# Four partial sums of a job: three merges, or one strided reduce of a PSUM bank

## The chip, the cores and the metric

The kernel runs on one core of a Trainium2 chip (trn2). The metric is the time of one launch on the device in microseconds. It was measured in three runs.

## The reference

A recommendation model. For each of 512 samples, 39 embeddings of 16 numbers are gathered from 39 tables. They go through three layers of a compressed interaction network, then through three dense layers. Cut to what matters here, with m = 39 fields, h = the previous layer's units (39, then 128) and 128 units out:

```python
prev = x                                   # [b, 39, 16]
for k in range(3):
    z = jnp.einsum('bmd,bhd->bdmh', x, prev).reshape(b, D, m * h)
    t = jnp.einsum('bdc,co->bdo', z, ws[k]) + bs[k]
    t = jnp.transpose(t, (0, 2, 1))
    norm = jnp.sqrt(jnp.sum(t * t, axis=(-2, -1), keepdims=True))
    t = t / norm
    logit.append(t)
    prev = t
```

For layers 1 and 2 this is, for each sample and embedding column, the sum over 39 fields m of x[m] times (prev row times the weight matrix of field m).

## The kernel before

The 512 samples are 16 chunks of 32; a chunk has 32 x 16 = 512 rows, four tiles of 128. A **job** is one tile of one chunk in layer 1 or 2; there are 128 jobs (`NJ`), interleaved: in iteration `it`, four jobs of layer 1 for chunk `it`, then four of layer 2 for chunk `it - 1`. So the loop repeats every 8 jobs.

In a job, TensorE multiplies the tile of prev with the weights of four fields at a time into one PSUM bank of 512 columns (four fields of 128 units), each bank with three matmuls (low by high, high by low and high by high halves, lines 554 to 556). Ten banks make the 39 fields. Five banks (19 fields) are the A half: ScalarE scales each field's 128 columns by that field's x column (`scale_bank`, line 441), into `sums` for the first bank and into `scaled` for the rest, and GpSimd adds them to `sums` (`add_bank`, line 333). The A banks have a ring of two PSUM banks, and TensorE is `LEAD` = 7 banks ahead with them.

The other five banks are the D half: 20 fields (`D_FIELDS`), numbered u = 0 to 19 here, field u in bank u // 4 at columns 128 x (u % 4), over a ring of three PSUM banks (`bank_d`). VectorE takes each field with one scalar_tensor_tensor (`add_field`, line 756): bank columns times the x column plus `sums[u % 4]`. It can begin field 0 only when GpSimd's four adds of the same job are done (`a_added`, line 749), since both use the four partial sums in `sums`. Field u of 4 and over waits for field u - 4.

At the end of a job four partial sums are left and have to become one. Fields 17 and 18 (`LEFT`) write their results back to their own columns of the bank. Field 19 adds to partial sum 0, which already has field 17's result. The **three merges** (`merge`, line 775) are: step 0, partial sum 0 = partial sum 0 + field 17's columns; step 1, field 18's columns = these + partial sum 3; step 2, partial sum 0 = partial sum 0 + field 18's columns. VectorE's program order is, by hand: field 18, steps 0 and 1, field 19, field 0 of the next job, step 2, field 1, and so on. TensorE waits for the semaphore `merged` in two places: before it writes the bank three D banks later (line 582), and before it transposes the total (`turn_sums`, line 591) into `turned`.

After a chunk's four tiles ScalarE adds the bias (`finish`), VectorE sums values and squares (`sum_values`, `sum_squares`, lines 779 and 783, tensor_reduce of 512 columns to 32), TensorE sums squares over partitions, ScalarE takes the root, and VectorE makes the reciprocal in four short steps (lines 793 to 804), placed between fields 1 to 4 of a later job. `make_prev` (line 821) then writes the next layer's prev, ScalarE copies its high half (`high`, line 481), and GpSimd makes the low half (`low`, line 338). ScalarE's program order has `high` between two scale_bank calls. Layer 0 goes by products of pairs of fields: VectorE multiplies them (`make_pairs`, line 734), and TensorE sums them with 14 matmuls a chunk (line 619). Every queue's order is written out by hand.

Of the kernel before, what the change touches and what calls it, by code (L numbers as in the profile page):

```python
# [8 lines left out]
UNITS = 128  # L9
# [27 lines left out]
PER_BANK = 4  # L37
A_BANKS = 5
BANKS = -(-FIELDS // PER_BANK)
D_BANKS = BANKS - A_BANKS  # L40
A_FIELDS = A_BANKS * PER_BANK - 1
D_FIELDS = FIELDS - A_FIELDS
ADDS = A_BANKS - 1


LEFT = (D_FIELDS - 3, D_FIELDS - 2)
TOTAL = (D_FIELDS - 4) % PER_BANK
MERGES = 3
A_RING, D_RING = 2, 3
SUMS = 5  # L50

# [8 lines left out]
NJ = len(JOBS)  # L60
# [76 lines left out]
def cin_kernel(nc, idx_in, base_in, table, ctx_t, w0a, w0b, w1, w2, b0, b1, b2,  # L137
               w_top1, b_top1, w_top2, b_top2, w_top3, out):
    f32, f32r, i32 = mybir.dt.float32, mybir.dt.float32r, mybir.dt.int32
    ALU, ACT, AX = mybir.AluOpType, mybir.ActivationFunctionType, mybir.AxisListType  # L140
# [4 lines left out]
    with ExitStack() as ctx:  # L145
        def sb(name, shape, dt=f32):
            return ctx.enter_context(nc.sbuf_tensor(name, shape, dt))

        def pb(name):
            return ctx.enter_context(nc.psum_tensor(name, [128, 512], f32))  # L150

        def sem(name):
            return ctx.enter_context(nc.semaphore(name))
# [29 lines left out]
        sums = sb("sums", [128, SUMS, PER_BANK, UNITS])  # L183
# [17 lines left out]
        bank_d = [pb(f"bank_d{n}") for n in range(D_RING)]  # L201
# [30 lines left out]
        d_added = sem("d_added")  # L232
        merged = sem("merged")
# [29 lines left out]
        def d_fields_of(d):  # L263
            return min(PER_BANK, D_FIELDS - d * PER_BANK)

        def d_count(n, d):

            return n * D_FIELDS + min(PER_BANK * (d + 1), D_FIELDS)

        def x_of(c, q, m):  # L270
            return x_col[:, c % 3, q, m:m + 1]
# [274 lines left out]
        def _(pe):  # L546
            def three_terms(bank, k, c, q, m, count):

                at = slice(q * COLS, (q + 1) * COLS)
                lo, hi = prev_lo[k][:, c % 2, at], prev_hi[k][:, c % 2, at]  # L550
                to = bank[:, 0:count * UNITS]
                w_h = w_hi[k][:, m:m + count, :].rearrange("p m u -> p (m u)")
                w_l = w_lo[k][:, m:m + count, :].rearrange("p m u -> p (m u)")
                nc.tensor.matmul(to, lo, w_h, start=True, stop=False)  # L554
                nc.tensor.matmul(to, hi, w_l, start=False, stop=False)  # L555
                return nc.tensor.matmul(to, hi, w_h, start=False, stop=True)  # L556
# [17 lines left out]
            def bank_for_dve(n, d):  # L574
                k, c, q = JOBS[n]
                at = D_BANKS * n + d
                if n == 0:
                    pe.wait_ge(w_lo_made[1], len(W_PIECES[1]))
                if at >= D_RING:
                    was, bank = divmod(at - D_RING, D_BANKS)  # L580
                    if bank == D_BANKS - 1:
                        pe.wait_ge(merged, MERGES * (was + 1))
                    else:
                        pe.wait_ge(d_added, d_count(was, bank))
                three_terms(bank_d[at % D_RING], k, c, q, A_FIELDS + d * PER_BANK,
                            d_fields_of(d)).then_inc(d_ready, 1)

            def turn_sums(n):

                k, c, q = JOBS[n]  # L590
                pe.wait_ge(merged, MERGES * (n + 1))
                if q == 0 and n >= TILES:
                    k, c, _ = JOBS[n - 1]
                    pe.wait_ge(squared, FINISH_NO[k, c] + 1)
                nc.tensor.transpose(turned[:, q * COLS:(q + 1) * COLS], sums[:, n % SUMS, TOTAL, :],  # L595
                                    identity[:, :]).then_inc(turn_done, 1)
# [59 lines left out]
            for n in range(NJ):  # L656
                d = a = 0
                for place, whose in enumerate(PATTERN):
# [10 lines left out]
                    if (n, place) in PAIR_MATMULS_AT:  # L669
                        c, tiles = PAIR_MATMULS_AT[n, place]  # L670
# [20 lines left out]
            for n in range(2):  # L691
                for k in range(3):
                    top1(n, k)
            turn_sums(NJ - 1)
            for k in range(3):
                top1(2, k)
# [22 lines left out]
        def _(dve):  # L719
# [19 lines left out]
            def taken(n, u):  # L739
                d, i = divmod(u, PER_BANK)  # L740
                return bank_d[(D_BANKS * n + d) % D_RING][:, i * UNITS:(i + 1) * UNITS]

            def add_field(n, u):
                k, c, q = JOBS[n]
                d, i = divmod(u, PER_BANK)
                if i == 0:
                    dve.wait_ge(d_ready, D_BANKS * n + d + 1)
                if u < PER_BANK:
                    dve.wait_ge(a_added, ADDS * (n + 1))
                elif u < D_FIELDS - 1:  # L750
                    dve.wait_ge(d_added, n * D_FIELDS + u + 1 - PER_BANK)
                else:
                    dve.wait_ge(merged, MERGES * n + 1)
                total = sums[:, n % SUMS, TOTAL if u == D_FIELDS - 1 else u % PER_BANK, :]

                nc.vector.scalar_tensor_tensor(  # L756
                    out=taken(n, u) if u in LEFT else total, in0=taken(n, u), scalar=x_of(c, q, A_FIELDS + u),
                    in1=total, op0=ALU.mult, op1=ALU.add).then_inc(d_added, 1)

            def merge(n, step):  # L760

                first, second = LEFT
                total = sums[:, n % SUMS, TOTAL, :]
                other = sums[:, n % SUMS, (D_FIELDS - 1) % PER_BANK, :]
                if step == 0:
                    dve.wait_ge(d_added, n * D_FIELDS + first + 1)
                    out, in0, in1 = total, taken(n, first), total
                elif step == 1:
                    dve.wait_ge(d_added, n * D_FIELDS + second + 1)
                    out, in0, in1 = taken(n, second), taken(n, second), other  # L770
                else:
                    dve.wait_ge(d_added, (n + 1) * D_FIELDS)
                    dve.wait_ge(merged, MERGES * n + 2)
                    out, in0, in1 = total, taken(n, second), total
                nc.vector.tensor_tensor(out=out, in0=in0, in1=in1, op=ALU.add).then_inc(merged, 1)  # L775

            def sum_values(k, c):
                dve.wait_ge(biased, FINISH_NO[k, c] + 1)
                nc.vector.tensor_reduce(dsum[:, k, :], bdim(t[:, k, :]), AX.X, ALU.add).then_inc(values_summed, 1)
# [34 lines left out]
            def make_prev(b, k, c):  # L814
                dve.wait_ge(r_step, (b + 1) * R_STEPS)
                if c:
                    dve.wait_ge(prev_lo_made[k], c)
                if c >= 2:

                    dve.wait_ge(d_ready, D_BANKS * (JOB_AT[k, c - 2, TILES - 1] + 1))  # L820
                nc.vector.tensor_tensor(out=bdim(prev[:, k - 1, :]), in0=bdim(t[:, k - 1, :]),
                                        in1=r[:, k - 1, :].unsqueeze(2).to_broadcast([128, CB, EMB]),
                                        op=ALU.mult).then_inc(prev_made[k], 1)
# [4 lines left out]
                                    in1=w0b_sb[0:PAIR_ROWS, full, :], op=ALU.add).then_inc(w0_folded, 1)  # L828
            last = PAIR_TILES - 1
            nc.vector.tensor_tensor(out=w0_sb[0:FIELDS, last, :], in0=w0_sb[0:FIELDS, last, :],  # L830
                                    in1=w0b_sb[0:FIELDS, last, :], op=ALU.add).then_inc(w0_folded, 1)
# [19 lines left out]
            for n in range(NJ):  # L851
                for u in range(D_FIELDS):
                    add_field(n, u)
                    if u == LEFT[1]:
                        merge(n, 0)
                        merge(n, 1)
                    if u == 0 and n:
                        merge(n - 1, 2)
                    for b, (items, _, _, at) in enumerate(NORMS):
                        if at and at[0] == n:  # L860
                            since = u - at[1]
                            if since in (0, 1, 2, 3):
                                reciprocal_step(b, since)
                            prevs = [(k + 1, c) for k, c in items if k < 2]
                            if since in (4, 5) and since - 4 < len(prevs):
                                make_prev(b, *prevs[since - 4])
                            if since == 6:
                                features(b)
                    for k, c, _, at in FINISHES:
                        if at == (n, u):  # L870
                            sum_values(k, c)
                        if at and at == (n, u - 3):
                            sum_squares(k, c)
                    if (n, u) in PAIRS_AT:
                        make_pairs(*PAIRS_AT[n, u])
            merge(NJ - 1, 2)
            sum_values(2, CHUNKS - 1)
            sum_squares(2, CHUNKS - 1)
            for step in range(R_STEPS):
# [61 lines left out]
```

## Time and profile before

| | us |
|---|---|
| median of 3 runs | 1101.58 |
| lowest, highest | 1101.01, 1102.05 |
| profiled execution | 1101.28 |
| its span, first to last instruction | 1099.6 |

Mean granted TensorE clock of the span: 0.992. Line numbers in a profile are those of the kernel. A row of a timeline gives start and duration in us; where several alike follow each other they are merged as "x4". Instructions of one engine overlap, so the distance from one start to the next is often shorter than a duration. In square brackets stands how long the engine was idle before and whom it waited for.

### The profile page before, as it was taken

What the parts mean: (1) busy time and instruction counts of PE and PEld (TensorE: products, weight loads), DVE (VectorE), ACT (ScalarE), POOL (GpSimd) and SP (SyncE); (2) the same over time, 40 slices, a digit from 0 to 9 for tenths busy, and PEclk for the clock granted to TensorE, in tenths of its full rate; (3) what the DMA queues carried; (4) which work ended last, traced back from release to release, by engine and by line L of the source; (5) the groups of instructions that cost most, each with busy time, mean ns of one, the idle gap of its engine ahead of it and who ended that gap; (6) DMA issues with size and microseconds to landing.
All of it is one profiled execution on the core that took longest, in us unless ns stands there. A gap on an engine that the chain in (4) does not pass through costs nothing.

```text
span 1099.6 us, 17904 instructions
## 1 busy us (share of the span) xinstructions
PE 1052.5 (96%) x4394; PEld 794.1 (72%) x4394; DVE 969.0 (88%) x3317; ACT 780.5 (71%) x2628; POOL 866.9 (79%) x726
## 2 busy tenths in 40 slices
PE   0798999999999999999999999999999999999999
PEld 0366687777778787777778777777777777788773
DVE  2467799998999999999999999999999999899892
ACT  3266586877768687776868777786868777688762
POOL 5587798888889888888888888888888888577660
PEclk9899999999999999999999999999999999999999
DMA  6503040110303011030303002030301203000000
GB/s 228 131 13 73 2 118 7 35 41 3 73 3 73 2 35 42 5 71 3 73 2 71 5 11 66 3 73 2 74 2 20 56 3 73 0 2 1 1 1 1
DMA packets 56735, 41.20 MB, mean 37 GB/s; under 512 B 37915, under 2 KB 40859, under 8 KB 56502
## 3 DMA queue, kind: packets, MB, share of 16 engines
q1 hardware_dynamic: 49145, 32.17, 12.5%
q10 hardware_dynamic: 2365, 6.60, 1.7%
q0 software_dynamic: 5120, 1.29, 1.3%
q8 instruction: 35, 0.57, 0.2%
q14 instruction: 70, 0.57, 0.2%
HBM read 38.09 MB, written 1.94 MB: 36 GB/s over the span
## 4 chain that ended last, share of the span: by engine, by line
PE 67%; POOL 21%; issue 6%; ACT 4%; DMA 1%; DVE 0%; SPq 0%; POOLq 0%; ACTq 0%
POOL sums L333 17%; PE bank_a L554 10%; PE bank_d L554 9%; PE acc L619 9%; PE bank_d L555 9%; PE bank_d L556 9%; PE bank_a L556 9%; PE bank_a L555 9%; POOL gathered L320 4%; ACT scaled L441 2%; PE turned L595 1%; ACT sums L441 1%; PE bank_a L684 1%; DMA x_pairs<-x_scratch 1%; PE bank_d L708 1%
## 5 line engine op out<-in xcount | busy, mean ns | idle before, releaser
L333 POOL TENSOR_TENSOR sums<-sums,scaled 128x512 f32<-128x512 f32 (+1 forms) x512 | 642.8, 1256 | 154.0 <-ACT scaled L441 119.3
L756 DVE SCALAR_TENSOR_TENSOR sums<-bank_d,x_col,sums 128x128 f32<-128x128 f32 x2304 | 654.8, 339 | 74.4 <-PE bank_d L556 58.8
L441 ACT ACTIVATE scaled<-bank_a,x_col 128x128 f32<-128x128 f32 x1920 | 550.6, 382 | 152.9 <-PE bank_a L556 144.4
L554 PE MATMUL bank_d<-w_hi,prev_lo 128*128 128x512 f32 x640 | 286.1, 447 | 1.2 <-DVE sums L775 0.9
L554 PE MATMUL bank_a<-w_hi,prev_lo 128*128 128x512 f32 (+1 forms) x640 | 274.5, 429 | 12.0 <-POOL prev_lo L338 6.3
L556 PE MATMUL bank_d<-w_hi,prev_hi 128*128 128x512 f32 x640 | 253.3, 396 | 0.0
L555 PE MATMUL bank_d<-w_lo,prev_hi 128*128 128x512 f32 x640 | 253.0, 395 | 0.0
L556 PE MATMUL bank_a<-w_hi,prev_hi 128*128 128x512 f32 (+1 forms) x640 | 246.2, 385 | 0.0
L555 PE MATMUL bank_a<-w_lo,prev_hi 128*128 128x512 f32 (+1 forms) x640 | 245.9, 384 | 0.0
L441 ACT ACTIVATE sums<-bank_a,x_col 128x128 f32<-128x128 f32 x512 | 146.1, 370 | 88.3 <-PE bank_a L556 88.3
L320 POOL DMA_INDIRECT gathered<-in_table,idx x160 | 177.2, 1107 | 31.9 <-issue 21.7
L554 PEld LDWEIGHTS bank_a<-w_hi,prev_lo 128*128 128x128 f32 x640 | 120.6, 188 | 66.0 <-issue 20.9
L554 PEld LDWEIGHTS bank_d<-w_hi,prev_lo 128*128 128x128 f32 x640 | 121.0, 189 | 42.0 <-DVE sums L756 8.7
L555 PEld LDWEIGHTS bank_a<-w_lo,prev_hi 128*128 128x128 f32 x640 | 121.1, 189 | 37.2 <-issue 13.7
L555 PEld LDWEIGHTS bank_d<-w_lo,prev_hi 128*128 128x128 f32 x640 | 121.7, 190 | 29.7 <-issue 10.8
L556 PEld LDWEIGHTS bank_d<-w_hi,prev_hi 128*128 128x128 f32 x640 | 121.0, 189 | 28.9
L556 PEld LDWEIGHTS bank_a<-w_hi,prev_hi 128*128 128x128 f32 x640 | 120.8, 189 | 22.7
L619 PE MATMUL acc<-z,w_sb 117*128 117x512 f32 (+1 forms) x224 | 115.9, 605 | 0.7 <-issue 0.7
L734 DVE TENSOR_TENSOR z<-x_pairs 117x1024 f32<-117x1024 f32 x64 | 106.8, 1672 | 5.1 <-DMA x_pairs<-x_scratch 4.9
L756 DVE SCALAR_TENSOR_TENSOR bank_d<-bank_d,x_col,sums 128x128 f32<-128x128 f32 x256 | 78.8, 348 | 0.0
L775 DVE TENSOR_TENSOR sums<-bank_d,sums 128x128 f32<-128x128 f32 x256 | 71.3, 279 | 0.4 <-DVE sums L756 0.4
L619 PEld LDWEIGHTS acc<-z,w_sb 117*128 117x128 f32 (+1 forms) x224 | 42.4, 195 | 15.0 <-issue 6.0
(59 smaller groups left out, 484.7 us busy)
## 6 DMA issues: line engine op xcount, KB each, us to landing
x_pairs<-x_scratch SPq DMA_DIRECT2D x141, 156.0 KB
x_pairs<-x_scratch SPq DMA_DIRECT2D x78, 78.0 KB
gathered<-in_table,idx POOLq DMA_INDIRECT x160
w_raw<-in_w ACTq DMA_DIRECT2D x2, 768.0 KB, 7.2
x_scratch<-gathered SPq DMA_DIRECT2D x16, 72.0 KB
w_raw<-in_w ACTq DMA_DIRECT2D x1, 1024.0 KB, 5.7
w_raw<-in_w ACTq DMA_DIRECT2D x1, 896.0 KB
w_raw<-in_w ACTq DMA_DIRECT2D x1, 832.0 KB
```

The source lines that it names most:

```text
L320: nc.gpsimd.indirect_dma_start(out=gathered[0:n, c % 2, j, :], out_offset=None, in_=table[:, :], in_offset=bass.IndirectOffsetOnAxis(ap=id ...
L333: nc.gpsimd.tensor_tensor(out=sums[:, n % SUMS, 0:w, :], in0=sums[:, n % SUMS, 0:w, :], in1=scaled[:, a - 1, 0:w, :], op=ALU.add).then_inc ...
L441: op = nc.scalar.activation(to[:, i, :], bank_a[at % A_RING][:, i * UNITS:(i + 1) * UNITS], ACT.Copy, scale=x_of(c, q, a * PER_BANK + i))
L554: nc.tensor.matmul(to, lo, w_h, start=True, stop=False)
L555: nc.tensor.matmul(to, hi, w_l, start=False, stop=False)
L556: return nc.tensor.matmul(to, hi, w_h, start=False, stop=True)
L595: nc.tensor.transpose(turned[:, q * COLS:(q + 1) * COLS], sums[:, n % SUMS, TOTAL, :], identity[:, :]).then_inc(turn_done, 1)
L619: mm = nc.tensor.matmul(acc0[:, :], w0_sb[0:rows, tile, :], z0[0:rows, tile, :], start=(tile == 0), stop=(tile == PAIR_TILES - 1))
L684: return nc.tensor.matmul(tops[n][:, :], w[:, n * 128:(n + 1) * 128], x, start=(k == 0), stop=(k == 3))
L734: nc.vector.tensor_tensor(out=z0[0:rows, tiles[0]:tiles[0] + count, :], in0=x_rep[0:rows, :].unsqueeze(1).to_broadcast([rows, count, ROWS] ...
L756: nc.vector.scalar_tensor_tensor(out=taken(n, u) if u in LEFT else total, in0=taken(n, u), scalar=x_of(c, q, A_FIELDS + u), in1=total, op0 ...
L775: nc.vector.tensor_tensor(out=out, in0=in0, in1=in1, op=ALU.add).then_inc(merged, 1)
```

## The change

The last four fields of a job, 16 to 19, all write their results into their own columns of the job's last bank. Each still adds its partial sum. The three merges are gone. In their place a single tensor_reduce reads the bank with the order of dimensions turned, so that the four columns of a unit, 128 columns apart, are added, and writes the 128 totals to partial sum 0. It stands where the third merge stood, behind field 0 of the next job. Field 19 now adds partial sum 3 and waits for field 15 as others wait for theirs. `merged` counts one for a job.

```diff
-LEFT = (D_FIELDS - 3, D_FIELDS - 2)
-TOTAL = (D_FIELDS - 4) % PER_BANK
-MERGES = 3
+assert D_FIELDS % PER_BANK == 0
+TOTAL = 0
...
                     if bank == D_BANKS - 1:
-                        pe.wait_ge(merged, MERGES * (was + 1))
+                        pe.wait_ge(merged, was + 1)
...
-                pe.wait_ge(merged, MERGES * (n + 1))
+                pe.wait_ge(merged, n + 1)
...
-                elif u < D_FIELDS - 1:
+                else:
                     dve.wait_ge(d_added, n * D_FIELDS + u + 1 - PER_BANK)
-                else:
-                    dve.wait_ge(merged, MERGES * n + 1)
-                total = sums[:, n % SUMS, TOTAL if u == D_FIELDS - 1 else u % PER_BANK, :]
+                total = sums[:, n % SUMS, u % PER_BANK, :]
 
                 nc.vector.scalar_tensor_tensor(
-                    out=taken(n, u) if u in LEFT else total, in0=taken(n, u), scalar=x_of(c, q, A_FIELDS + u),
+                    out=taken(n, u) if u >= D_FIELDS - PER_BANK else total, in0=taken(n, u), scalar=x_of(c, q, A_FIELDS + u),
                     in1=total, op0=ALU.mult, op1=ALU.add).then_inc(d_added, 1)
 
-            def merge(n, step):
...
-                nc.vector.tensor_tensor(out=out, in0=in0, in1=in1, op=ALU.add).then_inc(merged, 1)
+            def merge(n):
+
+                dve.wait_ge(d_added, (n + 1) * D_FIELDS)
+                bank = bank_d[(D_BANKS * n + D_BANKS - 1) % D_RING]
+                nc.vector.tensor_reduce(sums[:, n % SUMS, TOTAL, :], bank.rearrange("p (i u) -> p u i", u=UNITS),
+                                        AX.X, ALU.add).then_inc(merged, 1)
...
                     add_field(n, u)
-                    if u == LEFT[1]:
-                        merge(n, 0)
-                        merge(n, 1)
                     if u == 0 and n:
-                        merge(n - 1, 2)
+                        merge(n - 1)
...
-            merge(NJ - 1, 2)
+            merge(NJ - 1)
```

## Rows read from the trace of the kernel before

**Rows 1.** The page, part 1: busy time and instructions of each engine.

```profile
PE 1052.5 (96%) x4394; PEld 794.1 (72%) x4394; DVE 969.0 (88%) x3317; ACT 780.5 (71%) x2628; POOL 866.9 (79%) x726
```

**Rows 2.** Busy us by stretches of one period: stretch, length, engines, clock, DMA.

```profile
454.90:486.50 31.60, 31.48 (x142) 25.32 (x141) 31.23 (x118) 25.92 (x90) 28.13 (x24) 1.00 0.29 64
486.50:494.40 7.90, 7.90 (x33) 5.65 (x31) 7.27 (x21) 5.93 (x19) 7.03 (x7) 1.00 0.04 5
494.40:510.20 15.80, 15.80 (x64) 11.40 (x63) 15.63 (x51) 9.25 (x33) 13.37 (x12) 1.00 0.02 2
510.20:518.00 7.80, 7.80 (x38) 6.21 (x37) 5.96 (x22) 6.58 (x22) 5.50 (x6) 1.00 0.01 1
sum 63.10, PE 62.98 PEld 48.58 DVE 60.09 ACT 47.68 POOL 54.03; mean PE 15.74 PEld 12.15 DVE 15.02 ACT 11.92 POOL 13.51
```

**Rows 3.** Waits from 195 to 985 us: total us, times, longest.

```profile
ACT prev_hi L481 <- DVE prev L821: 13.0, 13, 1.8
...
PEld bank_a L554 <- ACT scaled L441: 12.1, 26, 0.6
...
DVE sums L756 <- POOL sums L333: 4.8, 12, 0.7
```

**Rows 4.** Timeline of VectorE, 533 to 538 us: start, duration, instruction.

```profile
533.02 0.28 DVE L775 TENSOR_TENSOR sums<-bank_d,sums 128x128 f32<-128x128 f32 x1
...
533.42 0.34 DVE L756 SCALAR_TENSOR_TENSOR sums<-bank_d,x_col,sums 128x128 f32<-128x128 f32 x1
534.09 0.35 DVE L756 SCALAR_TENSOR_TENSOR sums<-bank_d,x_col,sums 128x128 f32<-128x128 f32 x1 [0.33 <-POOL sums L333]
534.36 0.28 DVE L775 TENSOR_TENSOR sums<-bank_d,sums 128x128 f32<-128x128 f32 x1
534.56 0.60 DVE L756 SCALAR_TENSOR_TENSOR sums<-bank_d,x_col,sums 128x128 f32<-128x128 f32 x2
...
536.87 0.68 DVE L821 TENSOR_TENSOR prev<-t,small 128x512 f32<-128x512 f32 x1
```

**Rows 5.** Timeline of ScalarE in two periods, around the copy of prev.

```profile
474.48 0.63 ACT L481 ACTIVATE prev_hi<-prev 128x512 fp32r<-128x512 f32 x1 [0.92 <-DVE prev L821]
...
537.58 0.63 ACT L481 ACTIVATE prev_hi<-prev 128x512 fp32r<-128x512 f32 x1 [0.92 <-DVE prev L821]
538.12 0.86 ACT L441 ACTIVATE scaled<-bank_a,x_col 128x128 f32<-128x128 f32 x3
```

**Rows 6.** Timeline of TensorE, 538 to 539.6 us.

```profile
538.28 0.39 PE L555 MATMUL bank_d<-w_lo,prev_hi 128*128 128x512 f32 x1
538.51 0.40 PE L556 MATMUL bank_d<-w_hi,prev_hi 128*128 128x512 f32 x1
539.03 0.50 PE L554 MATMUL bank_a<-w_hi,prev_lo 128*128 128x512 f32 x1
```

**Rows 7.** Groups by line and shape, whole span: busy us, mean ns, idle before.

```profile
L775 DVE TENSOR_TENSOR sums<-bank_d,sums 128x128 f32<-128x128 f32 x256 | 71.3, 279 | 0.4 <-DVE sums L756 0.4
...
L779 DVE TENSOR_REDUCE dsum<-t 128x32 f32<-128x512 f32 x48 | 32.4, 674 | 9.7 <-ACT t L465 9.7
...
L821 DVE TENSOR_TENSOR prev<-t,small 128x512 f32<-128x512 f32 x32 | 21.7, 678 | 0.0
```

**Rows 8.** Timeline of VectorE at a reduce, 518 to 519.4 us.

```profile
518.30 0.67 DVE L783 TENSOR_REDUCE ssq<-squares 128x32 f32<-128x512 f32 x1
518.90 0.35 DVE L756 SCALAR_TENSOR_TENSOR bank_d<-bank_d,x_col,sums 128x128 f32<-128x128 f32 x1
519.16 0.28 DVE L775 TENSOR_TENSOR sums<-bank_d,sums 128x128 f32<-128x128 f32 x1
```

**Rows 9.** The pair products: ns min/median/max, first and last start, shapes.

```profile
L734 DVE TENSOR_TENSOR z<-x_pairs x64: 671/1386/2690, 35.4 to 947.2; 117x1024 f32<-117x1024 f32 x48, 78x512 f32<-78x512 f32 x16
```

**Rows 10.** Timeline of VectorE and TensorE behind the last job.

```profile
1075.86 0.29 DVE L775 TENSOR_TENSOR sums<-bank_d,sums 128x128 f32<-128x128 f32 x1 [0.22 <-DVE sums L756]
...
1078.94 0.27 PE L595 MATMUL turned<-identity,sums 128*128 128x128 f32 x1
```

More of the change, by code:

```diff
@@ L749, in add_field @@
                     dve.wait_ge(a_added, ADDS * (n + 1))
-                elif u < D_FIELDS - 1:
+                else:
                     dve.wait_ge(d_added, n * D_FIELDS + u + 1 - PER_BANK)
-                else:
-                    dve.wait_ge(merged, MERGES * n + 1)
-                total = sums[:, n % SUMS, TOTAL if u == D_FIELDS - 1 else u % PER_BANK, :]
+                total = sums[:, n % SUMS, u % PER_BANK, :]
                 nc.vector.scalar_tensor_tensor(
-                    out=taken(n, u) if u in LEFT else total, in0=taken(n, u), scalar=x_of(c, q, A_FIELDS + u),
+                    out=taken(n, u) if u >= D_FIELDS - PER_BANK else total, in0=taken(n, u), scalar=x_of(c, q, A_FIELDS + u),
                     in1=total, op0=ALU.mult, op1=ALU.add).then_inc(d_added, 1)
-            def merge(n, step):
[L762 to L774, printed above, removed]
-                nc.vector.tensor_tensor(out=out, in0=in0, in1=in1, op=ALU.add).then_inc(merged, 1)
+            def merge(n):
[3 more added lines that the diff above has]
+                                        AX.X, ALU.add).then_inc(merged, 1)
             def sum_values(k, c):
```

## The prediction

> **What bounds the kernel now.** I read the busy times of the engines first, then the same by stretches of one period of the loop, then the waits of the long middle, then the order of instructions in the place where these waits meet. TensorE is busy 96% of the span and VectorE 88% [rows 1]. The loop repeats every 8 jobs: the copy that makes the high half of prev starts at 474.48 and again at 537.58, 63.10 us later [rows 5]. In such a period TensorE is busy 62.98 of 63.10 us and VectorE 60.09 [rows 2]. So TensorE leaves nothing to win in the middle: 0.12 us a period by that row, some 2 us in all. Another engine matters only where TensorE waits for it.
>
> The stretches [rows 2] show where that is. In the first 31.6 us (four jobs) VectorE is busy 31.23 us, and TensorE loses its 0.12 us there. The waits name the place: ScalarE waits about 1 us for prev once in a period (13.0 us, 13 times), VectorE 0.4 us for GpSimd's sums (4.8 us, 12 times), and TensorE's weight loads for bank_a wait for ScalarE's scaling [rows 3].
>
> Put in order, this is one chain. GpSimd's last add of a job lets VectorE begin field 0 of that job, at 534.09 after 0.33 us of waiting. Behind field 0 stand, in program order, the third merge of the job before (534.36), field 1 (534.56), more fields with the reciprocal steps between them, and make_prev at 536.87 [rows 4]. ScalarE sits idle 0.92 us until prev is there, copies it at 537.58, and only then, at 538.12, scales the bank that TensorE wants back [rows 5]. TensorE's next matmul into bank_a starts at 539.03, 0.52 us behind the one before it, where the steady distance is 0.23 [rows 6]. So 0.29 us of TensorE is lost there now, and whatever delays VectorE between 534.36 and 536.87 should add to it one for one. In this place VectorE is on the path, although TensorE is the bound elsewhere.
>
> **The change, part by part.** Instructions of VectorE overlap, so I count from start to start. The first two merges of a job take 533.02 to 533.42, the third 534.36 to 534.56: 0.20 us each, 0.60 us a job [rows 4], for 128 jobs (384 merges, of which the 256 that write sums have one row [rows 7]). Removed: 0.60 us a job.
>
> Added: one tensor_reduce a job that reads 512 columns and writes 128. The nearest rows are this kernel's own reduces of 512 columns to 32, 674 ns each [rows 7]; one starts at 518.30 and its successor at 518.90, 0.60 us [rows 8]. So 0.60 out and 0.60 in: VectorE's busy time gains nothing.
>
> Those reduces read SBUF side by side; the new one reads PSUM, with the four terms of each sum 128 columns apart. From below: a 128-column add is 279 ns and a 512-column multiply 678 [rows 7], so 384 more columns cost 399 ns, 1.04 ns a column, and 512 columns 0.53 us. From above: the pair products are the only VectorE work here whose rate changes; their median is 1386 ns and the slowest of the same shape takes 2690 [rows 9], about a factor of two. At twice the time per column the reduce would take 0.53 + 0.60 = 1.13 us. I take 0.60, from the row that is the same operation with the same count read: the multiply of 512 columns, which has PSUM among its inputs (r, each value read 16 times), is 678 ns against the reduce's 674 out of SBUF alone [rows 7], so neither PSUM nor a pattern other than side by side has a price in these rows.
>
> The Trainium skill, in "Advanced Engine Details and Errata", section PSUM Cachelines, says that PSUM's lines are 8 bytes and that a pattern that isn't contiguous slows matmuls significantly; of VectorE it says nothing there. The Trainium skill's "VectorE: DVE Perf Modes", section "Mode 1× (REGULAR) — the baseline", has it the other way: this mode assumes nothing and takes strange strides and PSUM operands. No row of before shows a strided read of PSUM.
>
> Fields 16 and 19 now write their bank in place of sums. A field that writes sums takes 534.09 to 534.36 [rows 4], one that writes the bank 518.90 to 519.16 [rows 8]: no cost. TensorE's waits on merged count to 1 in place of 3 and are met by the same event, the last step of the job. That event stays at its distance from field 18: before, field 18, two merges, field 19, field 0 and a merge are 0.26 + 0.20 + 0.20 + 0.26 + 0.26 + 0.20 = 1.38 us; after, 3 x 0.26 + 0.60 = 1.38. DMA queues, ScalarE and GpSimd issue what they issued.
>
> What moves is work past field 0. Before, two merges stood ahead of field 0 of the next job and one behind it; after, none ahead and 0.60 us behind. Where field 0 waits for nothing, it starts 0.40 us earlier and field 1 when it did. Where field 0 waits for GpSimd, it can't start earlier; the two merges used to be done before the wait was over, and now 0.40 us more stands behind it. In the stretch of rows 4: field 19 would start at 533.02, field 0 still at 534.09, the reduce at 534.36, field 1 at 534.96 and not 534.56, make_prev at 537.27, the high half at 537.98, the matmul at 539.43. Queued behind the reduce on VectorE are field 1, the reciprocal steps and make_prev; ScalarE waits for make_prev, TensorE for ScalarE. None of them has slack, so TensorE loses 0.40 us more there, has no idle time later in the period to make it up [rows 2], and the period becomes 63.5 us.
>
> How often: field 0's wait is there 12 times and ScalarE's 13 times [rows 3]. I take 13: 13 x 0.40 = 5.2 us.
>
> The ends: in the last job the last merge starts at 1075.86 and takes 0.29 us, and the transpose that reads it starts at 1078.94 [rows 10], behind matmuls that don't need it, so over 2 us of cover remain there, and in that job the order gives 1.29 us from field 18 before (0.26 + 0.40 + 0.34 + 0.29) and 1.27 after (0.26 + 0.34 + 0.67). At the start I count nothing. Sum: 1101.28 us of the profiled execution (span 1099.6) + 5.2 = 1106.5; the median of the runs, 1101.58, is 0.3 above it, so 1106.8.
>
> **The rivals.** *Covered after all.* The reduce goes at the rate of the rows and the shift is taken up, for instance because GpSimd, with fewer writes to SBUF beside it, reaches its last add sooner. For it: 0.60 against 0.60. Against: ScalarE's wait and TensorE's late start stand in the rows. It gives 1101.6, within a microsecond.
>
> *The strided read is slow.* At 1.13 us a reduce, VectorE has 8 x 0.53 = 4.2 us a period more and 3.0 free (63.10 - 60.09), so the period grows by at least 1.2. By stretches [rows 2], as three banks carry little work from one to the next, the excess over the time there is: 31.23 + 4 x 0.53 - 31.60 = 1.75; 7.27 + 0.53 - 7.90, none; 15.63 + 2 x 0.53 - 15.80 = 0.89; none in the last: 2.6 us. Over 15 periods this is 18 to 40 us, 1120 to 1141. From 0.98 us a reduce on (0.60 + 3.0 / 8) VectorE is the bound of the whole period; in the first four jobs, where it has 0.37 us free, a tenth more a reduce is enough. I set it at 1134; a rate between, 0.8 us, adds at rows 4's place 0.60 and in the full stretches 0.4, some 8 to 15 us. If the Trainium skill's rule on PSUM lines held for VectorE, it would be this case.
>
> *Faster.* If the reduce came in at 0.53 us, and TensorE won back its 0.12 us and part of its 0.29 us in each period because no shift came, it gives 1098. Against it: only two instructions a job fewer, and their time is replaced.
>
> *It doesn't do what it says*: 384 merges become 128 reduces by the code; this is not open.
>
> **How the numbers follow.** Forecast 1106.8 (0.5% slower), chance 0.45, its own range 1104 to 1110; covered 0.20; slow read 0.30, from 1110 to 1143; faster 0.05. The low end, 1100.5, takes in the covered case, the high end, 1141, most of the slow read. A measurement of this kernel can tell about 0.2%, 2.2 us, from no change. Slower by more than that: 0.45 and 0.30, less a little, 0.73. Within it 0.22. Faster 0.05.
>
> **What would show it.** A mean of the reduce near 0.67 us and its successor 0.60 us behind its start confirm the price; 1.2 us is the slow read. In the place of rows 4, field 1 starting 0.87 us behind field 0 and not 0.47, ScalarE waiting 1.3 us for prev and not 0.92, TensorE's gap before bank_a 0.9 us and not 0.52 confirm the shift, and a period of 63.5 us the sum; VectorE's busy time in a period should stay near 60. If the reduce costs 0.60 us and the period stays at 63.1, the step on the shift is wrong. If TensorE waits for bank_d all over the first four jobs, the slow read decides.

## The result and the profile after

The changed kernel takes 1106.48 us (median of 6 runs, 1104.44 to 1106.99), the kernel before beside it 1101.39 us. The ratio is 1.0042, 95% interval 1.0029 to 1.0055: slower by 0.4%. The forecast was 1106.8. The profiled execution has a span of 1104.5 us, 4.9 more than before.

First the page: busy time and instructions of each engine, then the groups of the reduce and of the fields that now write their bank (busy us, mean ns of one, idle before).

```profile
PE 1055.1 (96%) x4394; PEld 792.2 (72%) x4394; DVE 969.0 (88%) x3061; ACT 780.6 (71%) x2628; POOL 867.1 (79%) x726
...
L753 DVE SCALAR_TENSOR_TENSOR bank_d<-bank_d,x_col,sums 128x128 f32<-128x128 f32 x512 | 145.3, 347 | 14.5 <-PE bank_d L555 14.5
...
L761 DVE TENSOR_REDUCE sums<-bank_d 128x128 f32<-128x512 f32 x128 | 86.7, 677 | 0.0
```

256 instructions fewer on VectorE, and its busy time is 969.0 us to the digit, as in [rows 1]. The strided reduce out of PSUM takes 677 ns, the one out of SBUF 674 [rows 7].

One period after, from busy time by stretches (length; busy us of PE, PEld, DVE, ACT, POOL), against the sum in [rows 2]:

```profile
458.05:521.55 63.50, 63.23 (x272) 48.53 (x271) 60.03 (x191) 47.68 (x164) 53.96 (x46) 1.00 0.15 33
```

VectorE's 60.03 us are the 60.09 of before, and the period is 0.40 us longer. The waits of the middle, as [rows 3]:

```profile
PEld bank_a L553 <- ACT scaled L440: 12.4, 25, 0.6
PEld bank_d L553 <- DVE sums L753: 11.8, 35, 0.6
DVE sums L753 <- POOL sums L332: 9.0, 24, 1.2
...
ACT prev_hi L480 <- DVE prev L808: 16.7, 12, 1.8
```

ScalarE waits 1.4 us a time for prev and not 1.0. VectorE's field 0 waits for GpSimd twice in a period now, 24 times and not 12. The place itself, on VectorE's timeline, as [rows 4]:

```profile
535.65 1.12 DVE L753 SCALAR_TENSOR_TENSOR bank_d<-bank_d,x_col,sums 128x128 f32<-128x128 f32 x4
537.22 0.35 DVE L753 SCALAR_TENSOR_TENSOR sums<-bank_d,x_col,sums 128x128 f32<-128x128 f32 x1 [0.45 <-POOL sums L332]
537.49 0.68 DVE L761 TENSOR_REDUCE sums<-bank_d 128x128 f32<-128x512 f32 x1
538.08 0.60 DVE L753 SCALAR_TENSOR_TENSOR sums<-bank_d,x_col,sums 128x128 f32<-128x128 f32 x2
...
540.39 0.68 DVE L808 TENSOR_TENSOR prev<-t,small 128x512 f32<-128x512 f32 x1
```

The four fields run through, field 0 waits, and between it and field 1 there are now 0.86 us (537.22 to 538.08) where there were 0.47. make_prev starts 3.17 us behind field 0 and not 2.78. ScalarE and TensorE behind it, as [rows 5, 6]:

```profile
477.62 0.63 ACT L480 ACTIVATE prev_hi<-prev 128x512 fp32r<-128x512 f32 x1 [1.32 <-DVE prev L808]
...
541.11 0.63 ACT L480 ACTIVATE prev_hi<-prev 128x512 fp32r<-128x512 f32 x1 [1.33 <-DVE prev L808]
...
540.92 0.40 PE L555 MATMUL bank_a<-w_hi,prev_hi 128*128 128x512 f32 x1
541.39 0.50 PE L553 MATMUL bank_d<-w_hi,prev_lo 128*128 128x512 f32 x1
541.73 0.39 PE L554 MATMUL bank_d<-w_lo,prev_hi 128*128 128x512 f32 x1
541.96 0.40 PE L555 MATMUL bank_d<-w_hi,prev_hi 128*128 128x512 f32 x1
542.56 0.50 PE L553 MATMUL bank_a<-w_hi,prev_lo 128*128 128x512 f32 x1 [0.21 <-ACT scaled L440]
542.90 0.39 PE L554 MATMUL bank_a<-w_lo,prev_hi 128*128 128x512 f32 x1
...
541.39 0.19 PEld L553 LDWEIGHTS bank_d<-w_hi,prev_lo 128*128 128x128 f32 x1 [0.51 <-DVE sums L753]
```

ScalarE waits 1.33 us and not 0.92, the copies are 63.49 us apart and not 63.10. TensorE, at 0.23 us a matmul elsewhere, has 0.47, 0.34, 0.60 and again 0.34 us here between starts. The last row is the weight load of the matmul at 541.39: it waited for VectorE to give back its bank.

### The profile page after: what moved, and what is told of

It reads as the page before. It is cut to its first block, busy times and chain, and to the rows that moved or that the text cites. A ratio compares the mean times of both kernels' runs of the same rounds, so it can differ in the third digit from the quotient of the medians.

```text
span 1104.5 us, 17520 instructions
## 1 busy us (share of the span) xinstructions
PE 1055.1 (96%) x4394; PEld 792.2 (72%) x4394; DVE 969.0 (88%) x3061; ACT 780.6 (71%) x2628; POOL 867.1 (79%) x726
## 4 chain that ended last, share of the span: by engine, by line
PE 60%; POOL 21%; issue 5%; DVE 5%; ACT 5%; DMA 2%; SPq 0%; POOLq 0%; ACTq 0%; DVEq 0%
POOL sums L332 16%; PE acc L618 9%; PE bank_a L553 8%; PE bank_d L553 8%; PE bank_a L555 8%; PE bank_a L554 8%; PE bank_d L555 8%; PE bank_d L554 8%; POOL gathered L319 5%; ACT scaled L440 4%; DVE sums L753 2%; DVE prev L808 1%; DVE sums L761 1%; PE turned L594 1%; PE bank_a L683 1%
## 5 line engine op out<-in xcount | busy, mean ns | idle before, releaser
L753 DVE SCALAR_TENSOR_TENSOR sums<-bank_d,x_col,sums 128x128 f32<-128x128 f32 x2048 | 580.1, 337 | 64.8 <-PE bank_d L555 46.1
L753 DVE SCALAR_TENSOR_TENSOR bank_d<-bank_d,x_col,sums 128x128 f32<-128x128 f32 x512 | 145.3, 347 | 14.5 <-PE bank_d L555 14.5
L761 DVE TENSOR_REDUCE sums<-bank_d 128x128 f32<-128x512 f32 x128 | 86.7, 677 | 0.0
```

The costliest lines, as they stand in the source:

```text
L753: nc.vector.scalar_tensor_tensor(out=taken(n, u) if u >= D_FIELDS - PER_BANK else total, in0=taken(n, u), scalar=x_of(c, q, A_FIELDS + u), ...
L761: nc.vector.tensor_reduce(sums[:, n % SUMS, TOTAL, :], bank.rearrange("p (i u) -> p u i", u=UNITS), AX.X, ALU.add).then_inc(merged, 1)
```

## The experiments

The theory of the place says: the reduce costs as much as the merges, and the loss is that 0.40 us more of it stand behind a field 0 that waits. Its rival says that the reduce costs by itself, by its length, its reads or its hold on the bank. The periods below are the distance of ScalarE's copies of prev's high half in jobs 8k+2, as in [rows 5]. They are read from one period of each trace; a table behind the last experiment has thirteen periods of every kernel. The kernel before was measured beside each set of runs; its median was 1102.49 us beside the first four experiments, 1102.10 beside the next four and 1101.28 beside the last.

**The reduce ahead of field 0, in one job of a period.**

```diff
+AHEAD = range(10, 128, 8)
...
                 for u in range(D_FIELDS):
+                    if u == 0 and n in AHEAD:
+                        merge(n - 1)
                     add_field(n, u)
-                    if u == 0 and n:
+                    if u == 0 and n and n not in AHEAD:
                         merge(n - 1)
```

> The changed kernel with the reduce moved ahead of field 0 in one job of each period (jobs 10, 18, ... 122, the ones whose field 0 waits for GpSimd before make_prev); everywhere else it stays behind field 0. Theory of the place (what stands behind that field 0 is on the path): 0.60 us less behind field 0 than in the changed kernel, of which 0.40 is the loss of the change and 0.20 comes off the 0.29 us that TensorE lost in the kernel before; period 63.5 to 62.9 us, 13 x 0.60 = 7.8 us off 1106.5, so 1098 to 1100; ScalarE's wait for prev 0.7 us. Rival (the reduce itself costs, by its length, by how long it holds the bank or by its reads): 128 reduces are still there, 1105 to 1107.

Measured: 1102.01 us, ratio to before 0.9998 (0.9989 to 1.0007), so not the 1098 to 1100 expected. The loss of the change is gone with 15 of 128 reduces moved, which the rival can't explain. The further gain didn't come. VectorE's timeline of this kernel says why:

```profile
534.05 1.12 DVE L754 SCALAR_TENSOR_TENSOR bank_d<-bank_d,x_col,sums 128x128 f32<-128x128 f32 x4
535.21 0.69 DVE L762 TENSOR_REDUCE sums<-bank_d 128x128 f32<-128x512 f32 x1
535.81 0.86 DVE L754 SCALAR_TENSOR_TENSOR sums<-bank_d,x_col,sums 128x128 f32<-128x128 f32 x3
...
538.38 0.68 DVE L809 TENSOR_TENSOR prev<-t,small 128x512 f32<-128x512 f32 x1
```

Four fields start 1.03 us apart in all (4 x 0.26), so the reduce could start at 535.08 and starts at 535.21: it waits for field 19 right ahead of it. And field 0 carries no mark of a wait here: VectorE, not GpSimd, is last to come. It left job 8k+1 late, since field 0 waits there too, which is the second wait a period in the list above.

**The same with merges.** The diff is the one above in the kernel before, with `merge(n - 1, 2)`.

> The kernel before with the third merge moved ahead of field 0 in the same jobs (10, 18, ... 122). Theory of the place: 0.20 us less behind field 0, all of it inside the 0.29 us that TensorE loses there; period 63.1 to 62.9 us, 13 x 0.20 = 2.6 us off 1101.4, so 1098 to 1099.5. Rival (TensorE is the bound of the kernel before and VectorE's order is covered): 1101 to 1102.

Measured: 1099.08 us, ratio 0.9974 (0.9964 to 0.9983), the copies 62.88 us apart:

```profile
474.32 0.63 ACT L482 ACTIVATE prev_hi<-prev 128x512 fp32r<-128x512 f32 x1 [0.91 <-DVE prev L822]
...
537.20 0.64 ACT L482 ACTIVATE prev_hi<-prev 128x512 fp32r<-128x512 f32 x1 [0.70 <-DVE prev L822]
```

A kernel whose TensorE is busy 96% gets 0.26% faster by moving one 0.20 us instruction of VectorE past another, once in eight jobs. That is the mechanism with the sign turned.

**The same amount behind field 0, without a reduce.**

```diff
+            def extra(n):
+                dve.wait_ge(merged, MERGES * n + 2)
...
+                for half in range(2):
+                    nc.vector.tensor_tensor(out=spare[:, half, :], in0=taken(n, LEFT[1]),
+                                            in1=sums[:, n % SUMS, (D_FIELDS - 1) % PER_BANK, :],
+                                            op=ALU.add).then_inc(spare_made, 1)
...
+                    if u == 0 and n in MORE:
+                        extra(n - 1)
                     if u == 0 and n:
                         merge(n - 1, 2)
```

> The kernel before with two more 128-column adds, results unused, between field 0 and the third merge in the same jobs (10, 18, ... 122); no reduce of a bank. They put 0.60 us behind field 0 as the change does, with merges. Theory of the place: as the changed kernel, period 63.5 us, 13 x 0.40 = 5.2 us more, 1106 to 1107.5. Rival (the reduce itself costs): VectorE has 3 us free in a period, 0.40 more in one job is covered, 1101 to 1102.

Measured: 1107.48 us, ratio 1.0053 (1.0041 to 1.0065). The copies are 63.47 us apart, ScalarE waits 1.31 to 1.37 us:

```profile
476.69 0.63 ACT L484 ACTIVATE prev_hi<-prev 128x512 fp32r<-128x512 f32 x1 [1.37 <-DVE prev L836]
...
540.16 0.63 ACT L484 ACTIVATE prev_hi<-prev 128x512 fp32r<-128x512 f32 x1 [1.31 <-DVE prev L836]
```

The change's loss is copied with merges alone, over thirteen periods 5.38 us with them and 5.27 with the change.

**The same adds elsewhere in the period** (`MORE = range(15, 128, 8)`).

> The kernel before with the same two more adds at the same distance behind field 0, but in jobs 15, 23, ... 127, whose field 0 waits for TensorE's bank and behind which VectorE is idle. Theory of the place: TensorE's next need of these banks is 2 us off, nothing is lost, 1101 to 1102. Rival (any VectorE time added costs): 5 to 6 us as in the other kernel with more adds, 1106 to 1107.

Measured: 1103.12 us, ratio 1.0009 (1.0000 to 1.0019), the copies 63.12 us apart. The same work in a job where field 0 waits for TensorE costs 0.02 us in this period and not 0.37, and 0.7 us over thirteen periods and not 5.4. By the medians it is 0.6 us slower, at the edge of what can be told. The 1101 to 1102 expected was missed, mostly because the kernel before itself was at 1102.49 in this set.

```profile
475.77 0.63 ACT L484 ACTIVATE prev_hi<-prev 128x512 fp32r<-128x512 f32 x1 [0.97 <-DVE prev L836]
...
538.89 0.64 ACT L484 ACTIVATE prev_hi<-prev 128x512 fp32r<-128x512 f32 x1 [0.94 <-DVE prev L836]
```

**Field 0 without its wait, with merges and with the reduce.** The same edit in both kernels:

```diff
+SHORT = [n for n in range(9, 128) if n % 8 in (1, 2)]
...
-                w = a_fields_of(a)
+                w = a_fields_of(a) if a < A_BANKS - 1 or n not in SHORT else 1
```

> The kernel before with GpSimd's last add cut from 3 fields to 1 in two jobs of each period (9, 10, 17, 18, ...), so two fields' contributions of one bank are left out of those jobs' sums. It frees field 0 of these jobs about 0.6 us earlier, before VectorE gets to it. Theory of the place: field 0 waits no more, TensorE's 0.29 us goes, period 62.8 to 62.9 us, 1097 to 1099. Its main use is as the base for the next kernel.

> The changed kernel with the same cut of GpSimd's last add in the same jobs, the same contributions left out. Theory of the place: the 0.40 us was lost only because field 0 waited; without that wait field 0 starts 0.40 us earlier than with the merges and field 1 when it did, so this kernel is as fast as the kernel before with the same cut, within 1.5 us. Rival (the reduce costs by itself, or the distance behind field 0 costs with or without a wait): 5 us slower than it.

Measured: 1096.42 us with merges, ratio 0.9950 (0.9936 to 0.9963), and 1097.83 with the reduce, ratio 0.9957 (0.9943 to 0.9970). The difference of 5.1 us between the kernels has come down to 1.4, inside the 1.5 expected, though not to nothing. The first kernel gained a little more than expected; the part on TensorE's gap below has the reason. The copies of prev with merges, then with the reduce:

```profile
472.50 0.64 ACT L482 ACTIVATE prev_hi<-prev 128x512 fp32r<-128x512 f32 x1 [0.79 <-DVE prev L822]
...
535.23 0.63 ACT L482 ACTIVATE prev_hi<-prev 128x512 fp32r<-128x512 f32 x1 [0.49 <-DVE prev L822]
```

```profile
472.84 0.63 ACT L481 ACTIVATE prev_hi<-prev 128x512 fp32r<-128x512 f32 x1 [0.65 <-DVE prev L809]
...
535.65 0.63 ACT L481 ACTIVATE prev_hi<-prev 128x512 fp32r<-128x512 f32 x1 [0.65 <-DVE prev L809]
```

These are 62.73 and 62.81 us. With the reduce field 0 comes to its turn 0.40 us earlier, and a rest of the wait for GpSimd is left. In this trace the four fields start at 530.59, so field 0 could start 4 x 0.26 us later, at 531.63; it starts at 531.76:

```profile
530.59 1.13 DVE L754 SCALAR_TENSOR_TENSOR bank_d<-bank_d,x_col,sums 128x128 f32<-128x128 f32 x4
531.76 0.35 DVE L754 SCALAR_TENSOR_TENSOR sums<-bank_d,x_col,sums 128x128 f32<-128x128 f32 x1
```

13 times those 0.13 us are 1.7. In the two traces thirteen periods differ by 1.8 us (816.06 and 817.86), the medians by 1.4.

**The stride by itself.**

```diff
-bank.rearrange("p (i u) -> p u i", u=UNITS)
+bank.rearrange("p (u i) -> p u i", u=UNITS)
```

> The changed kernel with the reduce reading four columns side by side in place of four columns 128 apart, so it adds the wrong terms: the four partial sums of a unit are not what is added. All theories that have the strided read at full rate: the reduce takes 677 ns as before and the time is that of the changed kernel, 1105 to 1107.5. Rival (the stride has a price in it): the reduce gets shorter than 677 ns.

Measured: 1106.47 us, ratio 1.0038 (1.0026 to 1.0050), and the reduce is as long as before:

```profile
L761 DVE TENSOR_REDUCE sums<-bank_d 128x128 f32<-128x512 f32 x128 | 87.0, 679 | 0.0
```

A stride of 128 columns in PSUM had no price in this fp32 reduce of VectorE: 677 ns strided, 679 side by side, and the kernel isn't faster with the second.

**Both jobs with a wait mended.** `AHEAD = [n for n in range(9, 128) if n % 8 in (1, 2)]` in the first experiment's kernel.

> The changed kernel with the reduce ahead of field 0 in two jobs of each period, 8k+1 and 8k+2. With one job (8k+2) the period was 63.1 and not the 62.9 expected: the trace has VectorE come 0.2 us late out of job 8k+1, where field 0 waits for GpSimd too, and the reduce wait 0.1 us for field 19 right ahead of it. Theory: with the job before it mended as well, field 1 of job 8k+2 starts 0.2 us behind GpSimd's add less than before, period 62.9 to 63.0, 1099 to 1101. Rival (what is lost is the reduce's wait for field 19, twice now): 63.2 and over, 1103.

Measured: 1097.76 us beside 1102.10, ratio 0.9961 (0.9947 to 0.9974), faster than the 1099 to 1101 expected. The copies are 62.97 us apart, as expected, and ScalarE waits 0.79 us:

```profile
473.11 0.63 ACT L481 ACTIVATE prev_hi<-prev 128x512 fp32r<-128x512 f32 x1 [0.77 <-DVE prev L809]
...
536.08 0.63 ACT L481 ACTIVATE prev_hi<-prev 128x512 fp32r<-128x512 f32 x1 [0.79 <-DVE prev L809]
```

The idea of the change, placed right, beats both kernels, by less than the medians say. Of the 4.3 us between them thirteen periods explain 1.4. Another part is TensorE's clock and not the order of work: the mean granted clock was 0.994 in all five runs of this kernel, and 0.991 or 0.992 in all eleven of the kernel before beside it. In the kernel before that difference goes with 1.6 us (last section). The remaining 1.3 us stay open.

**Ahead of field 0 in every job.** `AHEAD = range(1, 128)`.

> The changed kernel with the reduce ahead of field 0 in every job from 1 on. In the two jobs of a period with a wait of field 0 this gained (period 62.97 against 63.50); in the other six the reduce now waits some 0.12 us for field 19 right ahead of it, and VectorE is nearly full there. Theory: that wait costs only where VectorE holds TensorE up, at most six times 0.12 in a period; VectorE's 0.6 us of idle time in the middle absorbs part: period 63.0 to 63.4, 1098 to 1103, no faster than with two jobs. Rival (the place behind field 0 costs in every job): faster than with two jobs, under 1097.

Measured: 1099.88 us, ratio 0.9984 (0.9975 to 0.9993), faster than before. By the ratios it gains less than with two jobs, but the periods don't show that: the copies are 63.00 us apart here and 62.97 there, and thirteen periods take 819.79 us here and 819.87 there. In the middle of the loop the two are the same, and the ratio of the other has its clock in it. So the reduce's place in the other six jobs costs nothing and gains nothing that these runs can tell. The reduce, whose group had no idle time before it in the changed kernel, now has 4.4 us of it:

```profile
L762 DVE TENSOR_REDUCE sums<-bank_d 128x128 f32<-128x512 f32 x128 | 88.5, 692 | 4.4
```

**Thirteen periods of every kernel.** One trace each, from a copy of prev's high half near 158 us to the one thirteen periods later. The rows are those of the kernel before, then of the changed kernel; the table has the same distance for all.

```profile
158.00 0.63 ACT L481 ACTIVATE prev_hi<-prev 128x512 fp32r<-128x512 f32 x1 [0.62 <-DVE prev L821]
...
979.28 0.63 ACT L481 ACTIVATE prev_hi<-prev 128x512 fp32r<-128x512 f32 x1 [0.73 <-DVE prev L821]
```

```profile
159.13 0.63 ACT L480 ACTIVATE prev_hi<-prev 128x512 fp32r<-128x512 f32 x1 [0.98 <-DVE prev L808]
...
985.68 0.63 ACT L480 ACTIVATE prev_hi<-prev 128x512 fp32r<-128x512 f32 x1 [1.13 <-DVE prev L808]
```

| kernel | from, to (us) | thirteen periods | against before |
|---|---|---|---|
| before | 158.00, 979.28 | 821.28 | |
| changed | 159.13, 985.68 | 826.55 | +5.27 |
| reduce ahead, one job | 159.63, 980.45 | 820.82 | -0.46 |
| third merge ahead, one job | 158.59, 977.70 | 819.11 | -2.17 |
| two more adds in the place | 158.21, 984.87 | 826.66 | +5.38 |
| two more adds elsewhere | 158.86, 980.87 | 822.01 | +0.73 |
| merges, without the wait | 158.05, 974.11 | 816.06 | -5.22 |
| reduce, without the wait | 157.93, 975.79 | 817.86 | -3.42 |
| reduce, side by side | 159.08, 986.19 | 827.11 | +5.83 |
| reduce ahead, two jobs | 157.26, 977.13 | 819.87 | -1.41 |
| reduce ahead, every job | 158.38, 978.17 | 819.79 | -1.49 |

## Why the prediction was right, and where it wasn't exact

*The price of the reduce.* Taken as 0.60 us from start to start, between bounds of 0.53 and 1.13. It is 0.59 (537.49 to 538.08), and VectorE's busy time didn't move. The choice by the row of the same operation held; the slow read, given 0.30, is refuted by the 677 ns and by the experiment on the stride. The Trainium skill's rule on PSUM's lines ("Advanced Engine Details and Errata", section PSUM Cachelines), which speaks of matmuls, doesn't carry over to VectorE here: 677 ns against 679. The section "Mode 1× (REGULAR) — the baseline" of "VectorE: DVE Perf Modes" in the Trainium skill, which takes strange strides and PSUM operands, agrees with these two numbers.

*The work that moves past field 0.* The step that made the forecast. Field 1 at 0.87 us behind field 0 was expected, it is 0.86; ScalarE's wait of 1.3 us is 1.33; the period of 63.5 us is 63.49. The kernel with extra adds in this place (1107.48) copies the loss without a reduce, the one with them elsewhere (1103.12) doesn't, and without field 0's wait 1.4 us are left of 5.1.

*TensorE's gap.* One gap of 0.92 us before bank_a was expected. There are two, 0.47 us before bank_d and 0.60 before bank_a. VectorE's delay hits TensorE first through the bank it has to give back, then through ScalarE. The path through bank_d was not in the prediction; the sum is the same, since both carry one delay. The prediction also left out that the second matmul behind a gap starts 0.34 or 0.35 us behind the first and not 0.23, in the kernel before too:

```profile
539.38 0.39 PE L555 MATMUL bank_a<-w_lo,prev_hi 128*128 128x512 f32 x1
```

So TensorE lost 0.29 + 0.12 = 0.41 us at the place before the change, and not 0.29. After it, it loses 0.24 + 0.11 + 0.37 + 0.11 = 0.83: 0.42 more, as the period says. The kernel with merges and without field 0's wait has no gap left there, and its period of 62.7 us is these 0.4 us shorter than 63.10.

*Field 0's other wait.* The prediction said field 0 starts 0.40 us earlier wherever it waits for nothing. In job 8k+1 it waits for nothing before, but has less than 0.40 us to spare: the trace after shows a second wait for GpSimd in each period. It cost nothing, since the longer wait in the next job took it up, but it is part of why the first experiment missed its further 0.2 us a period: with both jobs mended the period is 62.97 us, 0.1 below the 63.1 of one job. The rest may be the reduce's wait for field 19, which the trace still has; no run takes it away.

*The count and the ends.* 13 x 0.40 = 5.2 was the sum; thirteen periods of the traces differ by 5.27, and the medians by 5.1. Over the whole of the two profiled executions it isn't so neat. TensorE's matmul behind its last long wait starts at 1037.39 before and 1043.82 after: 6.4 us later, 1.2 more than the sum, which had nothing for the start and the end. The first copy of prev's high half comes at 49.99 before and at 50.50 after; no merge and no reduce has run by then, and over all eleven traces it comes between 49.51 and 51.47, so that half microsecond isn't the change's. Up to 158 us, and in the jobs behind the last period, some tenths each were lost. Then 1.5 us are given back, because TensorE's clock fell there in the execution before and not in the one after (below). The agreement to 0.3 us of the median is so in part luck; what is tested is the 0.40 us a period.

*The ends' cover.* The last reduce starts at 1080.29 and the transpose at 1083.93, so the cover of rows 10 held.

## What to carry to other kernels

When an instruction is exchanged for others of equal length, ask what it stands behind. In this kernel work ahead of a wait was nearly free up to the length of the wait, and the same work behind it was paid for in full, because the waiting engine was on the path there, although it was not the busiest engine. In a loop with a nearly full engine, look for the place in a period where it waits for a chain of others that has no slack. Here a reorder of 0.20 us at that place took 2.2 us off thirteen periods, while 0.40 us of added work elsewhere cost 0.7. When two versions differ by a few tenths of a per cent, compare the periods of their traces and the granted clock of their runs before the medians.

## What the runs showed of the hardware

TensorE's granted clock can fall behind one wait and not behind the same wait in another execution. Both kernels idle some 1.9 us for GpSimd's low half, at 1037 and 1043 us. Here are the matmuls that end the waits, before and after, and the stretches of 4.3 us behind them with the granted clock as the third number from the end:

```profile
1037.39 0.50 PE L554 MATMUL bank_a<-w_hi,prev_lo 128*128 128x512 f32 x1 [1.87 <-POOL prev_lo L338]
...
1037.30:1041.60 4.30, 4.21 (x11) 3.32 (x12) 1.61 (x7) 1.71 (x7) 1.00 (x2) 0.60 0.00 0
```

```profile
1043.82 0.50 PE L553 MATMUL bank_a<-w_hi,prev_lo 128*128 128x512 f32 x1 [1.86 <-POOL prev_lo L337]
...
1043.80:1048.10 4.30, 4.28 (x18) 3.49 (x19) 2.70 (x10) 2.77 (x10) 1.61 (x2) 1.00 0.00 0
```

Before, the mean is 0.60 of full speed, a part of the stretch at the lower level of 1.2 GHz; after, 1.00, all at 2.4. The first got 11 matmuls done and the second 18, which costs about 1.5 us.

All eleven traces have this wait, 1.85 to 1.88 us long. Behind it the clock falls in six (the kernel before, the reduce and the merge ahead in one job, the adds in the place, the reduce without the wait, the reduce side by side) and not in five. These six runs have a mean granted clock of 0.991 or 0.992, the five 0.994, so the mean tells for the runs without a trace too. Of the 29 runs of the kernel before beside the first four experiments, ten have 0.994 and take 1099.23 to 1101.60 us (median 1101.07), nineteen have less and take 1102.12 to 1103.87 (median 1102.67). So this is a large part of the scatter of one kernel's runs. The shares differ from kernel to kernel (none of eleven runs at 0.994 with the reduce ahead in one job, five of five in two jobs); whether the order of work decides that or chance does wasn't tested.
